# Dense bf16 products ahead of each stage's first wait, and the last feed-forward part's FP4 quantiser rewritten to run in turns

## The reference, cut to what matters

```
x = x + layernorm(part(layernorm(x)))
```

```
def fp4_quant_dequant(x):
    xb = x.reshape(shape[:-1] + (shape[-1] // 16, 16))
    scale = maximum(max(abs(xb), axis=-1) / 6.0, 1e-12)
    xn = xb / scale
    q = GRID[searchsorted(MID, abs(xn))] * sign(xn) * scale     # GRID 0, .5, 1, 1.5, 2, 3, 4, 6

gate = fp4_linear(x, w_gate); y = fp4_linear(x, w_up)           # 128 -> 352
h = silu(gate) * y
return fp4_linear(h, w_down)                                    # 352 -> 128; fp4_linear quantises its input too
```

## Time and profile before

| what | value |
|---|---|
| median of three runs | 3988.82 us (3984.69 to 3989.2) |
| the profiled execution | 3997.76 us, its span 3996.0 us |
| share of the span: PE, DVE, ACT, POOL | 74%, 61%, 38%, 19% |
| granted TensorE clock, mean of the span | 0.827 of 2.4 GHz |
| last l3f stage: from its first DVE instruction to the last h quantised | 3916.8 to 3981.5 us |

### The profile page before, as it was taken

The page is one execution under the profiler, slowest core; times in us unless marked ns, Lnnn a source line. Parts: engine busy times, 40 slices in busy tenths (PEclk is TensorE's granted clock), DMA queues, the critical chain, the costliest instruction groups (busy, mean ns, idle before and its releaser), DMA issues. The chain is left out here.

```text
span 3996.0 us, 89258 instructions
## 1 busy us (share of the span) xinstructions
PE 2953.4 (74%) x35522; PEld 2030.4 (51%) x35522; DVE 2448.1 (61%) x6802; ACT 1529.1 (38%) x3093; POOL 773.2 (19%) x823
## 2 busy tenths in 40 slices
PE   4667888886557788888654777988856487798884
PEld 3434565654444456565443445656534344465653
DVE  6675665557667557545756755654575775565457
ACT  4144444422414444442241544444324154344432
POOL 4122212101213221210121322121112132212110
PEclk7578999997657899889765889988966588898896
DMA  1011000000001100000000110000000011000000
GB/s 39 6 39 31 15 3 3 15 20 1 7 6 42 31 12 3 2 18 16 1 7 6 42 34 9 3 2 18 17 1 8 6 43 34 9 3 2 22 13 6
DMA packets 65269, 59.75 MB, mean 15 GB/s; under 512 B 16403, under 2 KB 54212, under 8 KB 64838
## 3 DMA queue, kind: packets, MB, share of 16 engines
q1 hardware_dynamic: 63606, 53.24, 4.9%
q10 hardware_dynamic: 1232, 0.61, 0.1%
HBM read 36.29 MB, written 2.10 MB: 10 GB/s over the span
## 5 line engine op out<-in xcount | busy, mean ns | idle before, releaser
L1254 POOL TENSOR_TENSOR l1t_ss<-l1t_ss,neghalf 128x16 f32<-128x16 f32 x64 | 243.1, 3798 | 461.0 <-DVE l1t_ss L1288 461.0
L167 POOL TENSOR_TENSOR ln_y_rstd<-ln_var_eps,neghalf 128x4 f32<-128x4 f32 x64 | 64.8, 1013 | 1092.3 <-DVE ln_var_eps L188 1056.5
L1464 PE MATMUL l1t_ring<-l1f_qkv,x_normT 128*128 128x512 f32 x384 | 232.2, 738 | 18.7 <-ACT x_normT L1159 10.5
L2179 ACT ACTIVATE l2r_P<-l2r_bank_score 128x512 f32<-128x512 f32 x320 | 173.7, 594 | 178.1 <-PE l2r_bank_score L1901 178.1
L2179 ACT ACTIVATE l2a_P<-l2a_bank_score 128x512 f32<-128x512 f32 x320 | 173.7, 594 | 172.4 <-PE l2a_bank_score L1901 172.4
L2071 DVE CUSTOM_DVE_ANT_0 l2r_masked<-l2r_bank_ring,l2r_neg_wide 128x512 bf16<-128x512 f32 (+1 forms) x256 | 148.7, 622 | 76.7 <-PE l2r_bank_ring L1870 76.4
L2071 DVE CUSTOM_DVE_ANT_0 l2a_masked<-l2a_bank_ring,l2a_neg_wide 128x512 bf16<-128x512 f32 (+1 forms) x256 | 148.9, 622 | 71.3 <-PE l2a_bank_ring L1870 70.0
L1870 PE MATMUL l2r_bank_ring<-l2r_k_head,l2r_q_head 32*128 32x128 f32 x2432 | 174.4, 284 | 19.9 <-DVE l2r_m L2071 9.9
L1901 PE MATMUL l2r_bank_score<-l2r_q_head,l2r_k_head 32*128 32x128 f32 x2560 | 186.7, 283 | 2.6 <-DMA l2r_q_head<-l2r_shiftT 1.2
L1901 PE MATMUL l2a_bank_score<-l2a_q_head,l2a_k_head 32*128 32x128 f32 x2560 | 186.0, 282 | 3.0 <-DMA l2a_q_head<-l2a_shiftT 1.6
L1870 PE MATMUL l2a_bank_ring<-l2a_k_head,l2a_q_head 32*128 32x128 f32 x2432 | 174.5, 284 | 16.7 <-DVE l2a_m L2071 7.1
(11 more groups left out here) (619 smaller groups left out, 7751.1 us busy)
## 6 DMA issues: line engine op xcount, KB each, us to landing
l1t_v_low<-l1t_v SPq DMA_DIRECT2D x112, 130.0 KB, 2.4
l2e_w<-in_L_ffn_w SPq DMA_DIRECT2D x96, 128.0 KB, 2.2
l1f_qkv<-in_L_ffn_wqkv SPq DMA_DIRECT2D x8, 768.0 KB, 4.4
l1f_tables<-in_l_tables SPq DMA_DIRECT2D x8, 512.0 KB, 5.9
l1f_w<-in_L_ffn_w SPq DMA_DIRECT2D x8, 341.0 KB
x_in<-in_L_attn_hidden_states SPq DMA_DIRECT2D x10, 256.0 KB, 3.5
l1f_wo<-in_L_ffn_wo SPq DMA_DIRECT2D x8, 256.0 KB, 4.7
l2a_q_head<-l2a_shiftT SPq DMA_DIRECT2D x128, 2.0 KB
```

Source lines behind the costliest of these rows:

```text
L167: pool.tensor_tensor((b.yrs if post else b.rs)[:, p, :], b.ve[:, p, :], b.neghalf[:, 0:NT], ALU.pow).then_inc(s["post_rstd"] if post else ...
L1254: pool.tensor_tensor(ss[:, n % 2], ss[:, n % 2], b.neghalf[:, 0:2 * H8], ALU.pow).then_inc(s["rn_ready"], 1)
L1464: pe.matmul(take(what, n)[:, :], hT[:, p, j * 128:(j + 1) * 128], lw.qkv[:, c * INNER:(c + 1) * INNER], start=True, stop=True)\
L2179: act.activation(self.P[:, use % self.P_RING].rearrange("k h q -> k (h q)"), self.score_bank(h, g)[:, :], ACT.Exp, scale=self.scale).then_ ...
```

## The change

Two things are changed.

`busy(pe, b, bank, count)` issues `count` products of a 128 x 128 bf16 identity with 512 columns of bf16 constants into a bank that the stage writes only later. It stands ahead of TensorE's first wait: 20 in l0f, 10 in l1a, 10 in l1t (d = 0 only), 10 in l2a, 12 in l2r, 10 in l2e, 10 in l3a, 20 in l3f. Its results are not read.

In l3f the quantiser is `fp4_in_turns`. It takes one or two jobs and issues each step for all jobs before the next step, and a step waits only for the step before of its own job. The magnitude (L836) and the sign step (L846) are gone; the value goes through the rounding with its sign. x is quantised as before, one job after the other. The eight h tiles go in groups (0), (1, 2), (3, 4), (5, 6), (7). The multiplication of h signals `h_ready`, and `gate_up` and Silu of a later tile wait for that instead of for `hq_ready`. TensorE turns x of p = 0, issues `gate_up(0)`, and then turns x of p = 1; afterwards it issues, per group, the `gate_up` of the next group, the turns of this one and its down products.

```diff
+def busy(pe, b, bank, count):
+
+    for _ in range(count):
+        pe.matmul(bank[:, :], b.ident_bf[:], b.neg["row_gt"][:].unsqueeze(1).to_broadcast([128, 4, 128]),
+                  start=True, stop=True)
...
+class Turns:
+    def __init__(self, eng, sem, n):
+        self.eng, self.steps, self.done = eng, Steps(eng, sem), [0] * n
+    def wait(self, i):
+        if self.done[i]:
+            self.eng.wait_ge(self.steps.sem, self.done[i])
+    def __call__(self, i, ins):
+        self.steps(ins)
+        self.done[i] = self.steps.n
+def fp4_in_turns(dve, turns, jobs, ready, dst_read=()):
+    block, unit = 16, 1.0 / 2
+    magic = 1.5 * 2.0 ** 23 * unit
+    def blocks(a):
+        return a.rearrange("p (n k) -> p n k", k=block)
+    def spread(a):
+        return a.unsqueeze(2).to_broadcast([a.shape[0], a.shape[1], block])
+    jobs = list(enumerate(jobs))
+    for i, (src, dst, am, inv, v, pw, r) in jobs:
+        turns.wait(i)
+        turns(i, dve.tensor_reduce(am, blocks(src), AX, ALU.max, apply_absolute_value=True))
...
+    for i, (src, dst, am, inv, v, pw, r) in jobs:
+        turns.wait(i)
+        turns(i, dve.tensor_tensor(r, r, pw, ALU.subtract))
+    for i, (src, dst, am, inv, v, pw, r) in jobs:
+        turns.wait(i)
+        if dst_read and dst_read[i][1]:
+            dve.wait_ge(*dst_read[i])
+        dve.tensor_tensor(blocks(dst), blocks(r), spread(am), ALU.mult).then_inc(ready, 1)
...
         @block.tensor
         def _(pe):
+            busy(pe, b, y[1], 20)
             transpose_x(pe, b, s["xq_ready"], s["xT_psum"], xq, bank)
...
-        scratch = [sb(f"q{k}", [128, PAIR, S]) for k in range(4)]
+        scratch = [sb(f"q{k}", [128, PAIR, S]) for k in range(3)]
...
+        groups = ((0,), (1, 2), (3, 4), (5, 6), (7,))
...
-                FP4(dve, step, b.xn[:, p].rearrange("p j d -> p (j d)"), xq[:, p].rearrange("p j d -> p (j d)"),
-                    am[:, p, :], inv[:, p, :], *[x[:, p, :] for x in scratch]).then_inc(s["xq_ready"], 1)
-            for n, (j, p) in enumerate(tiles):
-                dve.wait_ge(s["silu_ready"], n + 1)
-                dve.wait_ge(s["up_ready"], n + 1)
-                if n >= PAIR:
-                    dve.wait_ge(s["hq_ready"], n + 1 - PAIR)
-                    dve.wait_ge(s["hT_psum"], n + 1 - PAIR)
-                step(dve.tensor_tensor(h[:, p, :], silu[:, p, :], u_ps[p][:, 0:I_FFN], ALU.mult))
-                step.settle()
-                FP4(dve, step, h[:, p, :], hq[:, p, :], ham[:, p, :], hinv[:, p, :],
-                    *[x[:, p, 0:I_FFN] for x in scratch]).then_inc(s["hq_ready"], 1)
+                turns = Turns(dve, s["quant_own"], 1)
+                turns.steps.n = quant.n
+                fp4_in_turns(dve, turns, [(b.xn[:, p].rearrange("p j d -> p (j d)"), xq[:, p].rearrange("p j d -> p (j d)"),
+                                           am[:, p, :], inv[:, p, :], *[x[:, p, :] for x in scratch])], s["xq_ready"])
+                quant.n = turns.steps.n
+            for members in groups:
+                for n in members:
+                    p = tiles[n][1]
+                    dve.wait_ge(s["silu_ready"], n + 1)
+                    dve.wait_ge(s["up_ready"], n + 1)
+                    if n >= PAIR:
+                        dve.wait_ge(s["hq_ready"], n + 1 - PAIR)
+                    dve.tensor_tensor(h[:, p, :], silu[:, p, :], u_ps[p][:, 0:I_FFN], ALU.mult).then_inc(s["h_ready"], 1)
+                dve.wait_ge(s["h_ready"], members[-1] + 1)
+                turns = Turns(dve, s["quant_own"], len(members))
+                turns.steps.n = quant.n
+                fp4_in_turns(dve, turns, [(h[:, p, :], hq[:, p, :], ham[:, p, :], hinv[:, p, :],
+                                           *[x[:, p, 0:I_FFN] for x in scratch])
+                                          for p in (tiles[n][1] for n in members)], s["hq_ready"],
+                             [(s["hT_psum"], max(0, n + 1 - PAIR)) for n in members])
+                quant.n = turns.steps.n
...
+            def gate(n):
+                p = tiles[n][1]
                 act.wait_ge(s["gate_ready"], n + 1)
+                if n >= PAIR:
+                    act.wait_ge(s["h_ready"], n + 1 - PAIR)
                 act.activation(silu[:, p, :], g_ps[p][:, 0:I_FFN], ACT.Silu).then_inc(s["silu_ready"], 1)
-                if n >= 1:
-                    copy_h(n - 1)
-            copy_h(len(tiles) - 1)
+
+            gate(0)
+            for k, members in enumerate(groups):
+                for n in groups[k + 1] if k + 1 < len(groups) else ():
+                    gate(n)
+                for n in members:
+                    copy_h(n)
 
         @block.tensor
         def _(pe):
-            transpose_x(pe, b, s["xq_ready"], s["xT_psum"], xq, t_ps)
-            pe.wait_ge(s["xT_ready"], PAIR)
+            def turn_x(p):
+                pe.wait_ge(s["xq_ready"], p + 1)
+                for j in range(NT):
+                    last = pe.transpose(t_ps[p][:, j * 128:(j + 1) * 128], xq[:, p, j, :], b.ident[:])
+                last.then_inc(s["xT_psum"], 1)
 
             def gate_up(n):
                 j, p = tiles[n]
-                if n >= PAIR:
+                if j == 0:
+                    pe.wait_ge(s["xT_ready"], p + 1)
+                else:
                     pe.wait_ge(s["silu_ready"], n + 1 - PAIR)
                 pe.matmul(g_ps[p][:, 0:I_FFN], b.xT[:, p, j * 128:(j + 1) * 128], w["gT"][:],
                           start=True, stop=True).then_inc(s["gate_ready"], 1)
-                if n >= PAIR:
-                    pe.wait_ge(s["hq_ready"], n + 1 - PAIR)
+                if j:
+                    pe.wait_ge(s["h_ready"], n + 1 - PAIR)
                 pe.matmul(u_ps[p][:, 0:I_FFN], b.xT[:, p, j * 128:(j + 1) * 128], w["uT"][:],
                           start=True, stop=True).then_inc(s["up_ready"], 1)
 
-            gate_up(0)
-            for n, (j, p) in enumerate(tiles):
-                if n + 1 < len(tiles):
-                    gate_up(n + 1)
+            def turn_h(n):
+                p = tiles[n][1]
                 pe.wait_ge(s["hq_ready"], n + 1)
-                if n >= PAIR:
+                if n < PAIR:
+                    pe.wait_ge(s["xT_ready"], n + 1)
+                else:
                     pe.wait_ge(s["hT_ready"], n + 1 - PAIR)
                 for k, (c, rows) in enumerate(I_ROWS):
                     last = pe.transpose(t_ps[p][0:rows, k * 128:(k + 1) * 128], hq[:, p, c:c + rows], b.ident[:])
                 last.then_inc(s["hT_psum"], 1)
+
+            def down(n):
+                j, p = tiles[n]
                 pe.wait_ge(s["hT_ready"], n + 1)
                 for k, (c, rows) in enumerate(I_ROWS):
                     last = pe.matmul(y[p][:, j * D:(j + 1) * D], hT[0:rows, p, k, :], w["dT"][0:rows, k, :],
                                      start=k == 0, stop=k == 2)
                 if j == NT - 1:
                     last.then_inc(s["y_ready"], 1)
+
+            busy(pe, b, g_ps[0], 20)
+            turn_x(0)
+            gate_up(0)
+            turn_x(1)
+            for k, members in enumerate(groups):
+                for n in groups[k + 1] if k + 1 < len(groups) else ():
+                    gate_up(n)
+                for n in members:
+                    turn_h(n)
+                for n in members:
+                    down(n)
```

More of the change, by code:

```diff
@@ L870 @@
 FP4 = Quantizer(16, 6.0, 1e-12, 1.0 / 2, signed=False)
+class Turns:
[20 more added lines that the diff above has]
+        turns.wait(i)
+        turns(i, dve.tensor_scalar(am, am, 1.0 / 6.0, 1e-12, ALU.mult, ALU.max))
+    for i, (src, dst, am, inv, v, pw, r) in jobs:
+        turns.wait(i)
+        turns(i, dve.reciprocal(inv, am))
+    for i, (src, dst, am, inv, v, pw, r) in jobs:
+        turns.wait(i)
+        turns(i, dve.tensor_tensor(blocks(v), blocks(src), spread(inv), ALU.mult))
+    for i, (src, dst, am, inv, v, pw, r) in jobs:
+        turns.wait(i)
+        turns(i, dve.tensor_scalar(pw.bitcast(U32), v.bitcast(U32), EXPONENT, None, ALU.bitwise_and))
+    for i, (src, dst, am, inv, v, pw, r) in jobs:
+        turns.wait(i)
+        turns(i, dve.tensor_scalar(pw, pw, 1.0, magic, ALU.max, ALU.mult))
+    for i, (src, dst, am, inv, v, pw, r) in jobs:
+        turns.wait(i)
+        turns(i, dve.scalar_tensor_tensor(r, v, 1.0 - 2.0 ** -24, pw, ALU.mult, ALU.add))
+    for i, (src, dst, am, inv, v, pw, r) in jobs:
+        turns.wait(i)
+        turns(i, dve.tensor_tensor(r, r, pw, ALU.subtract))
+    for i, (src, dst, am, inv, v, pw, r) in jobs:
+        turns.wait(i)
+        if dst_read and dst_read[i][1]:
+            dve.wait_ge(*dst_read[i])
+        dve.tensor_tensor(blocks(dst), blocks(r), spread(am), ALU.mult).then_inc(ready, 1)
 def l0_ffn_weights(nc, ctx, b, a):
@@ L1024, in _ @@
         def _(pe):
+            busy(pe, b, k_ps[0], 10)
             transpose_xn(pe, b, s, y)
@@ L1443, in _ @@
             if d == 0:
+                busy(pe, b, y[1], 10)
```

(8 more changed lines are left out.)

1 line of the change is left out of this document (removed).

## The result

| | median | runs | ratio to before |
|---|---|---|---|
| before | 3986.76 us | 3982.78 to 3989.2 | |
| after | 3882.54 us | 3874.37 to 3890.85 | 0.9738, interval 0.9721 to 0.9755 |

The kernel became 104 us (2.6%) faster; forecast were 3908 us and a range from 3885. The profiled execution took 3877.94 us.

A forecast was written before the change was run, and what follows sets the result against it. DVE was taken to bound l3f between its ends, with TensorE idle at other boundaries. The profiled 3997.8 us less 67 (l3f) and 14 (products) gave 3917, or 3908 for the median, which lies 8.9 lower; range 3885 to 3950.

The forecast's parts named there:

- Bound and mechanism: DVE sets l3f's pace between its ends; independent turns start 0.44 us apart, not 0.56; PE idles at other boundaries.
- the front: Start of l3f: first h some 0.6 us after x's last step instead of 5.37, 4.8 us saved a stage.
- Rivals two to five: Turns overlap nothing: 3925, 0.12; TensorE bounds pairs: 3948, 0.15; dense products give no clock: 3936, 0.12; long stages slower: 4039, 0.05.
- The term for l3f: Last feed-forward part: 19.2 us of savings less 2.5 of losses, 16.7 us a stage, 67 us over four.
- quantiser of x: In l3f, removed sign and magnitude steps save about 1.0 us for each x, 2.0 for both.
- pairs and lone tiles: The h tiles in l3f: 10.8 us saved on three pairs at 7.05 us each, 1.6 on two lone tiles.
- wait for u of tile 2: Front of l3f: DVE waits 2.0 us at 1.2 GHz or none at 2.4; 1.5 charged.
- TensorE slow in pairs: Pairs in l3f: mostly 2.4 GHz expected, 1.0 us a stage charged for the rest; bound 10.5.
- less 2.5: Losses taken off l3f's 19.2 us: 1.5 for u of tile 2, 1.0 for TensorE slow in the pairs.
- the third rival: Pairs in l3f: clock stays at 0.50 and TensorE becomes the bound; 3948 us, chance 0.15.
- The products: Dense products at stage boundaries raise the clock for first projections: 3.6 us a turn of the loop, 14 in all.
- the condition that the prediction named: l1t's projections gain 1.8 us if the clock outlasts the wait for the tables' DMA.

The follow-up runs named there:

- padded pairs: Memset blocks ahead of four parts, in after and in after without products: 3911.6 against 3930.32 us (first pair), 3891.64 against 3924.92 us (second).

## Why the prediction fell short

**Bound and mechanism: right, but for the front.** DVE set the pace of l3f and still does; the turns overlap, rows 0.44 us apart; PE was idle at the boundaries. Rivals two to five did not come: no pair at 9 us, no TensorE bound, products that give rather than cost, no harm to the long parts.

**The term for l3f was undersized: 16.7 us a turn forecast, 19.0 found (76.2 / 4; 18.6 with the rewritten part alone).** In the last turn, where the whole is 18.6, step by step:

| term | forecast | found | from |
|---|---|---|---|
| quantiser of x | 2.0 | 2.1 | last step of x 13.65 us behind the start, 15.76 before |
| front, to the first h | 4.8 | 2.5 | 2.88 us against 5.37 |
| pairs and lone tiles | 12.4 | 13.8 | first h to last step of the last tile 29.2 us against 43.0 |
| wait for u of tile 2 | -1.5 | 0 | no idle time before it |
| TensorE slow in pairs | -1.0 | 0 | no idle time before any later h |
| sum | 16.7 | 18.4 | part 60.6 us against 79.2 |

The step of the prediction that failed is "less 2.5": both losses were charged, and neither came (0 us measured for each). The first was saved by the other error, the front that came 2.3 us late behind ScalarE's queue and so gave TensorE the time; the prediction followed gate and up to h, but not the Silu's place in its queue. That nothing was waited for there is luck, not foresight. The run with the Silu moved shows both: the front at 0.6 us, and waits of 1.1 us a turn against the 1.5 charged. For the second, the bound of the third rival took TensorE's whole chain of a pair at 1.2 GHz, while between 3838 and 3858 the clock was low only in part of 3844 to 3848 (0.56 and 0.59 in its two windows), and DVE never waited. Of the 1.4 us in the tiles, 0.7 are two short waits that before still had (5.4 in total, 4.7 of it at the front), and 0.6 the pairs at 6.86 instead of 7.05 us.

**The products: 14 us forecast, 20 found.** Per turn: l3a 2.1 against 1.0 (1.5 at two chances in three), l2a 1.6 against 0.6, l2r 0.7 against 0.3, l2e 0.5 against 0.7, l1t 0.1 against 1.2, l0f and l1a nothing, as forecast. The twenty in l3f, which the forecast left out, show as 1 to 2 us over the four turns (320.6 against 321.7, 245.5 against 247.3). (The prediction's own items give 5.6 x 2/3 = 3.7 a turn, where it says 3.6.) For l1t the condition that the prediction named failed: the clock did not outlast the wait for the tables (0.50 from 3118 on). In l3a only the first projections were counted; the low stretch behind the fillers (0.77), which also went, was not. The overrun past the first wait, 0.6 us in l3a, was forecast as up to 0.8.

**What stands outside the terms: 8.5 us.** The sum took every part that the change leaves alone as fixed. The first attention part alone differs by up to 8 us from turn to turn. Forecast and result differ by 23.7 us, taken against the part sums: 9.2 from l3f, 6.0 from the products, 8.5 from here. The range's low end, 20.2 a turn for l3f and 5.5 for the boundaries, held both terms; what it lacked was this difference, 2.5 us of which were needed. Nor was the base fixed: before itself came out at 3986.76 us in the runs beside after, 2.1 below the 3988.82 from which the forecast was counted.

## What to carry over

Two independent chains issued in turns on one in-order engine hide the distance between dependent instructions, if each waits only for its own step: here 6.86 us a pair instead of 8.78 with the same instructions. When one wait is taken from the head of a stage, look at the queue of every engine in the chain behind it, and not only at the producer: the Silu sat behind a copy that it did not need. When TensorE stands idle ahead of a stage, dense products that need nothing can pay where its real work follows directly (l3a 2.1 us a turn), and did not where the clock had fallen again during a wait for a DMA (l1t); and where the clock changes under a stage, its length scatters, so a range for the whole kernel needs that scatter too.

## What was not expected of the hardware

The same instructions took 103.4 or 106.4 us (l2e up to its last write) and 112 or 120 us (first attention part), with the granted clock as the only difference found in the rows: in one execution, 0.72 against 0.98 in one and the same stretch of two turns. With the products l3a was shorter and l2e longer in both padded pairs. And six extra products of 0.24 us, together with eight more at the head, made a stage 1.7 us shorter (235.7 against 242.5 in four turns, the Silu moved in both), since gate and up then went at 0.75 us for two instead of 1.38.
